# The routed experts' down products as three products of rounded halves

## What is computed

```python
logits = xf @ Wg                                  # 16 experts, top 2
for e in range(16):
    h = silu(xf @ W1[e] + b1[e]) * (xf @ W11[e] + b11[e])     # hidden 512
    y = y + (h @ W2[e] + b2[e]) * gates[:, e, None]
z = silu(xf @ Ws1 + bs1) * (xf @ Ws11 + bs11) @ Ws2 + bs2     # hidden 1024
out = x + tanh(g_ffn) * (y + z)
```

## Time and profile before

| | us |
|---|---|
| median of 3 runs | 576.16 (576.12 to 580.23) |
| the profiled execution | 570.58 |
| its span | 568.8 |
| TensorE busy | 547.2 (96%) |
| GpSimd busy | 326.7 (57%) |
| VectorE busy | 340.6 (60%) |
| ScalarE busy | 238.4 (42%) |
| down products of the routed experts, TensorE busy | 89.0 |

### The profile page before, as it was taken

One profiled execution on the slowest core, in us unless ns is written; L12 is line 12 of the kernel. 1 busy time (PEld: TensorE's weight loads), 2 busy tenths in 40 slices (PEclk: granted clock), 3 DMA queues, 4 the chain that ended last, 5 costly groups with the idle time before them and its releaser, 6 DMA issues.

```text
span 568.8 us, 11908 instructions
## 1 busy us (share of the span) xinstructions
PE 547.2 (96%) x3230; PEld 440.0 (77%) x3231; DVE 340.6 (60%) x846; ACT 238.4 (42%) x787; POOL 326.7 (57%) x267
## 2 busy tenths in 40 slices
PE   8879999999988999988999999999999999999997
PEld 6546666666657878877888888888888888888886
DVE  6556766756668853245555655566555655435687
ACT  0999899999895201202212221122212221233322
POOL 5577798898864286642375575354444650236660
PEclk9999999999999999999999999999999999999999
DMA  8671011011023145245358778557556210013442
GB/s 284 275 294 45 3 39 38 0 37 37 20 76 106 36 157 181 97 130 185 104 182 288 259 268 293 186 177 269 199 197 227 92 46 20 29 57 88 120 123 86
DMA packets 32897, 76.07 MB, mean 134 GB/s; under 512 B 4960, under 2 KB 21856, under 8 KB 29920
## 3 DMA queue, kind: packets, MB, share of 16 engines
q1 hardware_dynamic: 14960, 52.44, 26.1%
q10 hardware_dynamic: 14832, 14.82, 8.2%
q0 software_dynamic: 3072, 8.39, 4.8%
HBM read 54.93 MB, written 18.61 MB: 129 GB/s over the span
## 4 chain that ended last, share of the span: by engine, by line
PE 84%; ACT 7%; DVE 4%; issue 3%; POOL 1%; ACTq 0%; DVEq 0%; POOLq 0%
PE mid L709 14%; PE big L690 8%; PE big L692 8%; PE big L691 8%; PE big L611 5%; PE big L612 5%; PE big L613 5%; PE big L481 4%; ACT arena L797 4%; PE mid L700 4%; PE work L450 3%; PE mid L494 3%; PE work L513 3%; PE last L630 2%; PE last L506 2%
## 5 line engine op out<-in xcount | busy, mean ns | idle before, releaser
L895 ACT ACTIVATE last<-arena 128x512 f32<-128x512 f32 x47 | 28.3, 602 | 183.3 <-DVE arena L1346 183.3
L797 ACT ACTIVATE arena<-big,nmax 128x128 f32<-128x128 f32 x256 | 90.0, 388 | 3.2 <-DVE nmax L1017 3.1
L709 PE MATMUL mid<-dring,arena 128*128 x376 | 89.0, 379 | 0.0
L1346 DVE TENSOR_TENSOR arena<-big,bring 128x512 f32<-128x512 f32 x47 | 32.5, 691 | 88.9 <-PE big L692 88.9
L690 PE MATMUL big<-u_hi,xsT_hi 128*128 x188 | 81.9, 435 | 1.6 <-issue 1.6
L1509 POOL TENSOR_TENSOR u_lo<-arena,u_hi 128x2048 fp32r<-128x2048 f32 x16 | 74.3, 4642 | 1.3
L709 PEld LDWEIGHTS mid<-dring,arena 128*128 128x128 f32 x376 | 67.8, 190 | 7.3
L692 PE MATMUL big<-u_hi,xsT_lo 128*128 x188 | 73.5, 391 | 0.0
L691 PE MATMUL big<-u_lo,xsT_hi 128*128 x188 | 73.4, 391 | 0.0
L1485 POOL TENSOR_TENSOR arena<-arena,rinv 128x1024 f32<-128x1024 f32 (+1 forms) x32 | 58.6, 1832 | 23.1 <-DVE rinv L1025 23.0
L1595 POOL TENSOR_TENSOR pool_mark<-mhalf 128x1 f32<-128x1 f32 x15 | 2.9, 193 | 102.8 <-PE big L692 86.6
(11 more groups left out here) (173 smaller groups left out, 1141.2 us busy)
## 6 DMA issues: line engine op xcount, KB each, us to landing
arena<-up_w_dram SPq DMA_DIRECT2D x16, 1024.0 KB, 7.6
bring<-expert_bias_dram SPq DMA_DIRECT2D x16, 640.0 KB, 5.3
dring<-down_w_dram SPq DMA_DIRECT2D x18, 512.0 KB, 3.3
sorted_y<-arena ACTq DMA_DIRECT2D x47, 128.0 KB, 1.7
arena<-sorted_x ACTq DMA_DIRECT2D x43, 128.0 KB, 2.1
sorted_x<-dring SPq DMA_DIRECT2D x3, 1536.0 KB, 8.7
arena<-ctx_t_dram ACTq DMA_DIRECT2D x8, 256.0 KB, 2.6
dring<-up_w_dram SPq DMA_DIRECT2D x2, 1024.0 KB, 5.0
```

What stands on the lines that cost most here:

```text
L709: i = mm(mid[:, 1, 0:D], gT[:, p, c, :], dring[:, slot, c * D:(c + 1) * D], start=(c == 0), stop=(c == HC - 1))
L797: i = nc.scalar.activation(probs[:, u % 2, h, :], big[:, u % 2, h // 4, (h % 4) * CTX:(h % 4 + 1) * CTX], ACT.Exp, bias=nmax[:, u % 2, h:h ...
L1346: v.tensor_tensor(hb1[:, p, :], big[:, p, 0, :], bring[:, slot, 0:HID], ALU.add).then_inc(h1_ready, 1)
```

## The change

The down product `gT @ dring` becomes three fp32r products a chunk: `gT_hi @ w_hi`, `gT_hi @ w_lo`, `gT_lo @ w_hi`, all added up in PSUM. ScalarE's copy of the transposed hidden values now writes them rounded (`gT_hi`), and a new VectorE step, `keep_hidden`, writes the rest (`gT_lo`) from PSUM; `gT_ready` now counts that step. GpSimd splits the down weights too (`split_down`): a rounding copy and a subtraction for each expert, into a ring of two, `e_down`, which lies over the arena's buffer of the shared expert. The split of item i stands right behind the split of its up weights, and waits until `down_ps` has reached the end of expert i-2. The two first down splits stand around the up split of item 2, behind the shared expert's down products (`z_ps`). `down` waits for `e_split`. GpSimd's loop over experts is written out. The shared expert's VectorE step waits for `down_ps` before it writes into the buffer again.

```diff
+        e_down = sb("e_down", [P, 2, 2, DCOLS], F32R)
+        gT_hi = sb("gT_hi", [P, 2, HC, P], F32R)
+        gT_lo = sb("gT_lo", [P, 2, HC, P], F32R)
...
             def down(b, p):
-                slot = pe.snap(item_of(b) % WSLOTS)
+                item = item_of(b)
+                slot = pe.snap((item + 1) % 2)
+                pe.wait_ge(e_split, item)
                 pe.wait_ge(gT_ready, b + 1)
                 if not (isinstance(b, int) and b < 1):
                     pe.wait_ge(y_ready, b)
                 for c in range(HC):
-                    i = mm(mid[:, 1, 0:D], gT[:, p, c, :], dring[:, slot, c * D:(c + 1) * D], start=(c == 0), stop=(c == HC - 1))
+                    w_hi, w_lo = e_down[:, slot, 0, c * D:(c + 1) * D], e_down[:, slot, 1, c * D:(c + 1) * D]
+                    mm(mid[:, 1, 0:D], gT_hi[:, p, c, :], w_hi, start=(c == 0), stop=False)
+                    mm(mid[:, 1, 0:D], gT_hi[:, p, c, :], w_lo, start=False, stop=False)
+                    i = mm(mid[:, 1, 0:D], gT_lo[:, p, c, :], w_hi, start=False, stop=(c == HC - 1))
                 i.then_inc(down_ps, 1)
...
-                nc.scalar.activation(gT[:, p, :, :].rearrange("p c n -> p (c n)"), mid[:, 0, :], ACT.Copy).then_inc(gT_ready, 1)
+                nc.scalar.activation(gT_hi[:, p, :, :].rearrange("p c n -> p (c n)"), mid[:, 0, :], ACT.Copy).then_inc(gT_hi_ready, 1)
...
+                    if s == 4 and c == 0:
+                        dve.wait_ge(down_ps, BLOCKS - 1)
+                    if s == 5 and c == 0:
+                        dve.wait_ge(down_ps, BLOCKS)
...
+            def keep_hidden(b, p):
+                dve.wait_ge(gT_hi_ready, b + 1)
+                v.tensor_tensor(gT_lo[:, p, :, :].rearrange("p c n -> p (c n)"), mid[:, 0, :],
+                                gT_hi[:, p, :, :].rearrange("p c n -> p (c n)"), ALU.subtract).then_inc(gT_ready, 1)
...
                 if ahead:
                     hidden(n + 1, 1 - p)
+                keep_hidden(n, p)
                 add_out_bias(n - 1, 1 - p)
...
+            def split_down(i, before, slot):
+                source = dring[:, i % WSLOTS, :]
+                g.tensor_copy(e_down[:, slot, 0, :], source).then_inc(e_hi_done, 1)
+                pool.wait_ge(e_hi_done, before + 1)
+                g.tensor_tensor(e_down[:, slot, 1, :], source, e_down[:, slot, 0, :], ALU.subtract).then_inc(e_split, 1)
+
+            pool.wait_ge(w_odd, 32)
+            pool.wait_ge(z_ps, 3 * GROUP)
+            split_down(1, 0, 0)
             pool.wait_ge(raw_even, 16)
             pool.wait_ge(sh_ps, HC * TILES // GROUP)
             pool.wait_ge(split_done, 2)
             split(PIECES, raw[:, 0, :], 0, 0, 1)
+            pool.wait_ge(w_even, 64)
+            pool.wait_ge(z_ps, TILES)
+            split_down(2, 1, 1)
...
+            for i in range(3, ITEMS):
...
                 pool.wait_ge(up_ps, end)
                 g.tensor_tensor(pool_mark[:, :], mhalf[:, :], mhalf[:, :], ALU.mult)
                 split(PIECES + i - 2, raw[:, slot, :], slot, 0, 1)
+                if i < ITEMS - 1:
+                    pool.wait_ge(down_ps, end)
+                    g.tensor_tensor(pool_mark[:, :], mhalf[:, :], mhalf[:, :], ALU.mult)
+                    pool.wait_ge(w_odd if slot else w_even, 32 * (i // 2) + 32)
+                    split_down(i, i - 1, (i + 1) % 2)
```

More of the change, by code:

```diff
@@ L146, in flamingo_layer @@
         ARENA = 16128
-        arena = sb("arena", [P, ARENA])
+        with nc.sbuf_tensor("arena", [P, ARENA], F32) as whole:
+            arena = whole
+        e_down = sb("e_down", [P, 2, 2, DCOLS], F32R)
+        gT_hi = sb("gT_hi", [P, 2, HC, P], F32R)
+        gT_lo = sb("gT_lo", [P, 2, HC, P], F32R)
+        sb("arena_rest", [P, ARENA - 4 * DCOLS - 4 * HID])
         taken = [0]
@@ L171, in flamingo_layer @@
         gshT = part(2 * HC * 512).rearrange("p (s c n) -> p s c n", s=2, c=HC)
+        part(4 * HID)
         sil = part(2 * 512).rearrange("p (s n) -> p s n", s=2)
@@ L180, in flamingo_layer @@
         gg = part(2 * HID).rearrange("p (s n) -> p s n", s=2)
-        gT = part(2 * HID).rearrange("p (s c n) -> p s c n", s=2, c=HC)
         xs = part(XBUFS * D).rearrange("p (s n) -> p s n", s=XBUFS)
@@ L217, in flamingo_layer @@
         rinv = sb("rinv", [P, 2, HG])
+        gT_hi_ready = sem("gT_hi_ready")
         gT_ready = sem("gT_ready")
+        e_hi_done = sem("e_hi_done")
+        e_split = sem("e_split")
         kT_ready = sem("kT_ready")
@@ L1380, in _ @@
             hidden(1, 1)
+            keep_hidden(0, 0)
             for n in range(1, 5):
@@ L1587, in _ @@
             split(PIECES, raw[:, 0, :], 0, 0, 1)
+            pool.wait_ge(w_even, 64)
+            pool.wait_ge(z_ps, TILES)
+            split_down(2, 1, 1)
             pool.wait_ge(table_ready, 1)
-            def split_expert(i, slot):
-                pool.wait_ge(raw_odd if slot else raw_even, 8 * i + (8 if slot else 0))
-                end = pool.value_load(blk_end[0:1, bass.ds(i - USLOTS - 1, 1)], min_val=1, max_val=BLOCKS)
+            for i in range(3, ITEMS):
+                slot = i % USLOTS
+                pool.wait_ge(raw_odd if slot else raw_even, 16 * (i // 2) + 16 * slot)
+                end = pool.value_load(blk_end[0:1, i - USLOTS - 1:i - USLOTS], min_val=1, max_val=BLOCKS)
                 pool.wait_ge(up_ps, end)
```

## The result

The changed kernel takes 583.02 us (median of 7 runs, 577.67 to 587.07), the kernel before 576.19 (573.64 to 580.23). The ratio is 1.0112, with a 95% interval of 1.0085 to 1.0139: slower by 1.1%, 6.8 us by the medians, just past the bound of one percent, which lies inside the interval. The forecast was 577.8 in a range of 567 to 584. A later set of comparisons gave 1.0122 [1.0076, 1.0167]. Now and then an execution is some per cent slower than the others of its kernel, and the ratios leave those out.

What follows compares the result with a forecast made beforehand. TensorE, 96% busy, was the bound; its queue would take over. From 570.58 us profiled: products -14.1, loop slots +13.0, straight-line slots +1.3, GpSimd +1.2, start +0.2, giving 572.2; the median's 5.6 offset makes 577.8, range 567 to 584.

Steps and rivals of the forecast that it cites:

- rival 1: TensorE's busy time stays the bound, its queue covering the new waits: slots of 4.82, 567.1 us, chance 0.20.
- rival 2: TensorE's queue: e_split wait and register steps bring the addition to 1.6 us; slots of 5.38, 586.8 us, chance 0.15.
- the chain through TensorE's queue: Routed slots: lookups and register steps behind the hidden product, 10.25 or 10.45 us over two slots, 5.18 a slot.
- the 1.2: Time in us the change adds to TensorE's queue chain per pair of slots; bounds 0.9 and 1.6.
- subtraction: New VectorE step that TensorE's hidden transposes wait for; adds 0.61 us to the two-slot queue chain.
- register steps: TensorE's queue: eight instead of four for each down product, adding 0.50 us to the two-slot chain.
- the wait on e_split: One more wait in TensorE's queue before the down product, 0.1 us, between 0 and 0.2.
- The sum: All gains and losses of the change against the profiled 570.58 us: together +1.6, giving 572.2 in the profile.
- rival 3: GpSimd's late lookup of an expert's end makes its cycle 11.2 us, losing 4.2 instead of 1.2: 580.8, chance 0.15.
- edits with one answer: Remaining small edits, including first down splits, shared-step waits and moved buffers; only 0.2 us charged, before the first slot.
- GpSimd: Weight splits: a cycle of 10.6 us an expert against two slots of 10.36, losing 1.2 us over five two-block experts.
- TensorE's busy time: Total TensorE work in the changed kernel's profile, expected near 533 us as a sign the forecast was right.

Runs made afterwards that it cites:

- e8: Changed kernel without VectorE's new subtraction and the third product (hidden low half by weights' high half); ScalarE's copy releases TensorE. 561.26 us, ratio 0.9820 to the kernel before.
- e4: Changed kernel issuing only the first of the down product's three products, 4 matmuls instead of 12, splits and waits kept. 572.44 us, ratio 0.9904 to the kernel before.
- e1_up_first: Changed kernel with GpSimd's up split of item 2 moved ahead of both first down splits. 577.87 us, ratio 1.0028 to the kernel before.
- e10: Repeat on a third chip of the changed kernel with item 2's up split ahead of both first down splits. 577.62 us, ratio 1.0024 to the kernel before.
- e6: Kernel before, with GpSimd's up split of item 2 delayed behind the shared unit's third down group and an extra copy and subtraction. 577.81 us, ratio 1.0121.
- e5_no_down_splits: Changed kernel with up split first and early lookups, GpSimd's down splits of items 3 to 16 left out. 564.01 us, ratio 0.9864 to the kernel before.
- e2_lookup_early: Changed kernel with TensorE's down lookup, and in three of four slots the next up lookup, ahead of the hidden transposes. 575.49 us, ratio 0.9983 to the kernel before.

## Why the prediction came out as it did

The likeliest class, within one percent, had 0.55 and slower 0.20; the result is 1.1% slower, at the edge between them, and 5.2 us above the forecast. That is 1.0 inside the range of 567 to 584 and just outside the forecast's own range of 573 to 582. The wide range held because it had been drawn for rivals 1 and 2, and the cost that filled it is in neither: that much is luck.

**Right: the chain through TensorE's queue.** The forecast had 10.25 and 10.45 over two slots and 5.18 a slot; the rows give 10.13 and 10.42 (with the branch), holes of 0.42 and 0.68 ahead of every second L698, and 5.14. Taking the lookups out of the chain gains 7.5 us, and the same edit gains nothing in the kernel before. The parts of the 1.2: subtraction 0.61, measured 0.7 by e8 with the little that went beside it; register steps 0.50, measured 0.5 in the rows (0.96 from the first of eight to the last, instead of 0.45 for four) and 0.5 by e4; the wait on e_split 0.1, measured at nothing (0.75 from the lookup to the first register step, before and after). The Trainium skill's queue depth of 64 ("TensorE: Matmul & The Clock Gate", opening table) did not help here: in 37 of 46 slots the lookup starts 0.2 to 0.3 us after the subtraction waited for has ended, and in the other nine the queue comes to it later still.

**Right in total, for all but the collision.** e1_up_first is the changed kernel without it, and it stands at 1.0028 and 1.0024 of the kernel before, 1.4 to 1.6 us. The sum said 1.6, but the parts lie elsewhere. In the profiles the 44 slots of e1 and e10 take only 0.4 to 0.7 us more than before (225.24 and 225.51 against 224.86), and 1.4 lies between the third up product and the fourth, where the queue first comes late. The forecast had 0.2 ahead of the first slot and about 2 spread over all 45. So the closeness of the total is in part luck. Rival 1 (567.1) and rival 2 (586.8 by slots of 5.38) did not happen; the measured 583.0 lies close to rivals 2 and 3 for a reason that neither names.

**Wrong: "the first delays expert 2's up split from 249 to 257, used at 269"**, filed under edits with one answer and costed at nothing. The delay was larger, to 261.7, since the first down split waits for z_ps until 251.7, which the text did not look up. And the question put to it was only who needs the result. Nobody did by then; but the split still has to run, and what runs beside it at 257 is VectorE's gate arithmetic, in the chain. So the step that failed is the overlap, priced at nothing. The runs show 4.8 us between the sets of e1 and the changed kernel (0.84 points), 5.7 where the two ran side by side (0.98 points; 4.6 by the medians), and 6.9 by e6 alone.

**GpSimd** came in at 10.3 to 10.7 a cycle (10.6 forecast), with larger holes at the five two-block experts (slots of 6.20 and 5.81 among them). Ten slots took 52.8 there against 51.2 before, 1.6 where 1.2 was forecast.

**Sized wrong: TensorE's busy time**, put near 533 and shown as 548.7. L721 reads 0.28 where the next starts 0.12 later; the sum of rows with modelled ends is no measure of a gain.

**Not the change's:** of the 14.8 us between the two profiled spans, two stretches of 3.4 us at half clock in the attention part (20 and 37 us in; 3.2 us) and the late signals (about 1.8 at 240, and part of the 2.5 in the rest) are run and, as far as the sets tell, chip. Comparing those two profiles alone would have laid them on the change.

## What to carry to other kernels

When a step is moved behind a wait on a queue, ask not only who needs its result but what will run beside it on the engines that share something with it: a GpSimd subtraction of 4.6 us that slid by 13 us under a 0.23 us VectorE operation cost about three times as much as the whole rest of the change. Where an engine is 96% busy, look at its instruction queue before counting on shorter products: the lookups and register steps behind the last unmet wait form a chain of their own, and moving them ahead of that wait turned a change that lost 1.1% into one that gains 0.9 to 1.1%, once the split was back in its place. And undo one part at a time: the parts added up to within 0.1 points.

## What the runs showed of the hardware

- A VectorE operation of 128x16 was held for 4.3 to 4.4 us in six profiles, each time until 0.03 to 0.04 us after GpSimd's running two-operand subtraction ended.
- After the pause of some 2.7 us that this made on TensorE, its granted clock was at the lower level for 3.4 to 10.2 us in all six. Of eight profiles without the long operation one (e5_no_down_splits) had 3.4 us of it there.
- TensorE's queue did not start a table lookup placed behind an unmet wait: it came 0.2 to 0.3 us after the subtraction's end in 37 of 46 slots. With the lookups ahead of the wait (e2_lookup_early) the 44 slots took 7.15 us less.
- The same kernel took 571.1, 576.6 and 576.7 us on three chips, nearly 1%, as much as the effect under study. The ratios of the three kernels that ran in two sets agreed to 0.2 points; in each pair the kernel before took 576 to 577, and none of them ran on the chip of 571.1.
